# Moving the extra messages of a window from the end of its own pass to the head of the next one

## The reference

```python
h = (x @ W).reshape(n_nodes, Hh, Cc)
alpha = leaky_relu(a_src[src] + a_dst[dst])
m = jax.ops.segment_max(alpha, dst, num_segments=n_nodes)
e = jnp.exp(alpha - m[dst])
denom = jax.ops.segment_sum(e, dst, num_segments=n_nodes)
w = e / jnp.clip(denom, 1e-16)[dst]
out = jax.ops.segment_sum(w[:, :, None] * h[src], dst, num_segments=n_nodes)
```

## Time and profile before

| | |
|---|---|
| median of three runs | 6508.33 us |
| the profiled execution | 6517.74 us, its span 6515.9 us |
| PE busy | 4981.0 us (76%) |
| DVE busy | 5313.4 us (82%) |
| ACT busy | 2717.7 us (42%) |
| POOL busy | 4585.1 us (70%) |
| mean granted clock of PE | 0.775 of full |

### The profile page before, as it was taken

The page is one execution under the profiler, slowest core; times in us unless marked ns, Lnnn a source line. Parts: engine busy times, 40 slices in busy tenths (PEclk is TensorE's granted clock), DMA queues, the critical chain, the costliest instruction groups (busy, mean ns, idle before and its releaser), DMA issues. The chain is left out here.

```text
span 6515.9 us, 110173 instructions
## 1 busy us (share of the span) xinstructions
PE 4981.0 (76%) x21652; PEld 3682.0 (57%) x21653; DVE 5313.4 (82%) x16735; ACT 2717.7 (42%) x4351; POOL 4585.1 (70%) x4837
## 2 busy tenths in 40 slices
PE   6788888888888577777777777758778778787876
PEld 5555655555556355555555555536656556566653
DVE  6788888888888788888888888877778778777788
ACT  3333333333333245554545455533333333333335
POOL 2777777777776577776767676737777777777764
PEclk8777877877777678777777777767777777778786
DMA  8555555555555455555555555535555555555545
GB/s 274 149 156 156 157 157 155 157 156 156 156 155 141 117 162 160 160 159 156 159 158 162 153 162 157 162 102 161 160 158 161 160 159 161 160 160 160 160 131 159
DMA packets 505894, 1027.11 MB, mean 158 GB/s; under 512 B 146891, under 2 KB 313199, under 8 KB 504878
## 3 DMA queue, kind: packets, MB, share of 16 engines
q0 software_dynamic: 226208, 633.50, 36.2%
q1 hardware_dynamic: 278798, 382.44, 18.1%
HBM read 931.37 MB, written 84.15 MB: 156 GB/s over the span
## 5 line engine op out<-in xcount | busy, mean ns | idle before, releaser
L1032 POOL DMA_INDIRECT e_rows<-table,loaded x4689 | 4489.2, 957 | 1756.8 <-issue 1392.6
L1266 PE MATMUL e_p_mm<-e_rows,e_onehot 128*128 128x264 f32 x9378 | 2466.5, 417 | 0.0
L1266 PEld LDWEIGHTS e_p_mm<-e_rows,e_onehot 128*128 128x128 f32 x9378 | 1876.3, 208 | 360.5 <-issue 20.1
L1444 DVE TENSOR_TENSOR e_rows<-e_rows,e_p_pair 128x1024 f32<-128x1024 f32 x1173 | 1417.8, 1209 | 0.0
L1436 DVE TENSOR_TENSOR e_onehot<-e_col,e_p_pair 128x512 f32<-128x512 f32 (+1 forms) x1467 | 953.4, 650 | 328.2 <-issue 280.4
L1259 PE MATMUL e_p_mm<-e_xmsg,e_onehot 128*128 128x264 f32 x1764 | 875.3, 669 | 103.3 <-ACT e_p_mm L1133 86.2
L1274 PE MATMUL e_p_one<-ad_parts,e_onehotT 128*128 x5586 | 707.8, 188 | 149.6 <-issue 143.3
L1225 ACT ACTIVATE e_rows<-e_gap 128x64 f32<-128x64 f32 (+1 forms) x294 | 80.6, 274 | 1621.0 <-DVE e_gap L1766 1614.7
L1274 PEld LDWEIGHTS e_p_one<-ad_parts,e_onehotT 128*128 128x128 bf16 x5586 | 550.4, 102 | 330.4 <-issue 193.3
L1139 ACT ACTIVATE e_onehotT<-e_onehotT,minus_pidx 128x2432 bf16<-128x2432 bf16 x294 | 681.0, 2316 | 42.0 <-DMA e_pass<-pass_rows 42.0
L1142 ACT ACTIVATE e_onehotT<-e_onehotT,one_col 128x2432 bf16<-128x2432 bf16 x294 | 682.6, 2322 | 9.6
(11 more groups left out here) (326 smaller groups left out, 5819.3 us busy)
## 6 DMA issues: line engine op xcount, KB each, us to landing
e_onehotT<-rel_rows SPq DMA_DIRECT2D x294, 608.0 KB
e_rows<-table,loaded POOLq DMA_INDIRECT x4689
e_own_row<-table SPq DMA_DIRECT2D x196, 128.0 KB
table<-e_rows_out SPq DMA_DIRECT2D x98, 132.0 KB
table<-n_rows_out SPq DMA_DIRECT2D x14, 910.0 KB, 15.6
table<-e_rows_out SPq DMA_DIRECT2D x98, 130.0 KB
n_inputs<-in_x_turned SPq DMA_DIRECT2D x14, 896.0 KB, 11.2
e_mask<-mask_rows SPq DMA_DIRECT2D x196, 64.0 KB
```

The source lines that it names most:

```text
L1032: pool.indirect_dma_start(rows[k][:, g, 0:TW], None, table[L], bass.IndirectOffsetOnAxis(ap=idx[k][:, g:g + 1], axis=0)).then_inc(s_gat[k] ...
L1266: ins = nc.tensor.matmul(p_mm[:, bass.ds(region, MW)], onehot[:, g, :], rows[k][:, g, :], start=False, stop=True, skip_group_check=True)
L1444: return nc.vector.tensor_tensor(feats, feats, p_e[:, gs, :].unsqueeze(3).to_broadcast([P, n, H, C]), ALU.mult)
```

## The change

`extras()` of a window is no longer the last thing of the window's own pass but the first DVE work of the next one, behind the table loads of that pass; the words `slots` are read there as well, and no longer ahead of `quarters(3)`. Its buffer and its semaphore counts are those of the window before. The last window's extra messages are made behind the loop.

```diff
                     if not first:
                         off, = words(dve, WINDOW_ROW, (w - 1) * WIN, 1, (PLACES - 1) * ACC_W)
+                        slots = words(dve, WINDOW_ROW, (w - 1) * WIN + W_TILE, EXTRAS, G - 1)
                         if not second:
                             offs = words(dve, WINDOW_ROW, (w - 2) * WIN, REGIONS, (PLACES - 1) * ACC_W)
                     flag, = words(dve, WINDOW_ROW, w * WIN + W_FLAG, 1, 2)
...
+                    if not first:
+                        extras((k - 1) % BUFS, slots, past, ago(2))
                     dve.wait_ge(s_ld[two], count(dve, used(u, i, TURNS) * N_LOAD))
 
                     dve.wait_ge(st["srcT"], now)
...
-                    slots = words(dve, WINDOW_ROW, w * WIN + W_TILE, EXTRAS, G - 1)
                     quarters(3)
                     if CARRY:
                         carried(w, u, i)
-                    extras(k, slots, now, past)
...
                 offs = words(dve, WINDOW_ROW, (WINDOWS - 1) * WIN, REGIONS, (PLACES - 1) * ACC_W)
+                slots = words(dve, WINDOW_ROW, (WINDOWS - 1) * WIN + W_TILE, EXTRAS, G - 1)
                 flag, = words(dve, WINDOW_ROW, (WINDOWS - 1) * WIN + W_OWN, 1, 1)
+                extras(k, slots, done, done - 1)
                 rescale(offs[0], done)
```

## The result

| | before | after |
|---|---|---|
| median, run side by side | 6509.72 us (6507.12 to 6517.74, 4 runs) | 6581.49 us (6576.14 to 6583.16, 4 runs) |
| ratio | | 1.0107, 95% interval [1.0089, 1.0125] |
| profiled execution, its span | 6517.74, 6515.9 us | 6571.58, 6569.8 us |
| mean granted clock of PE | 0.775 | 0.780 |

The change makes the kernel 72 us slower by the medians (54 by the two profiled executions). The forecast was 6556 us in a range up to 6578: the side and the place are right, the size is not. Of the executions of the kernel before that ran beside the experiments, one took 11598 us and stands in no ratio.

What follows compares the result with a forecast made beforehand. POOL was taken to bound the first and third layers, DVE's order the second. Second layer +39, first +8, third 0 and tails +1 gave +48 us, put on the median: 6556 us, the forecast's own range 6538 to 6572, 8-in-10 range 6522 to 6578.

Steps and rivals of the forecast that it cites:

- What bounds each layer: POOL's gathers pace the first and third layer at 20.1 to 20.3 us a window; DVE's order the second, 21.5 us.
- rival A: Loads ahead of the extras run while carried() still waits, both gaps vanish: second layer -120 us, 6388 us; chance 0.06.
- rival B: Slots' load takes 0.755 us for its old place, not its three words; 0.35 in the new: 6512 us; chance 0.10.
- First and third layer, tails: First layer +8 us, DVE passing POOL by 0.12 us a window; third layer 0; tails behind the loops about +1.
- The second layer's +39 us: Second layer: five ordinary windows at +0.51 us and one turn's end at +0.1 average 0.44 us, times 88 windows.
- The ordinary window: Second layer: four loads open 2.1 us ahead of the extras, less gaps of 0.76 and 0.83 saved: +0.51 us.
- Rival C: Second stop of 0.8 us stays open at turns' ends, and a moving 0.18 us stop is added: 6590 us; chance 0.10.
- A turn's end: Second layer, window at the loop's branch: 7.77 us from L1554 to scan, less 7.0 and 0.76: called +0.1 us.
- The median: The +48 us from the profile was put on the median, 9.4 us below the profiled execution: 6556 us, not 6566.

Runs made afterwards that it cites:

- e1: The change, with the slots' tiles read as four aligned words, the fourth unused, in place of three; 6534.6 us, ratio 1.0032.
- c1_before: The kernel before once more, nothing changed; 6512.9 us, ratio 0.9996.
- c0_change: The change once more, no edit; 6580.0 us, ratio 1.0103 to the kernel before.
- e12: The change, but the slots' load stays ahead of the last quarter in five of six windows, so only the extras move; 6563.6 us, ratio 1.0077.
- e5c: Kernel before, slots' load moved behind quarters(2), three opening loads read at the end of the window before in five of six windows; 6419.8 us, ratio 0.9857.
- e3: The change, with the four loads behind the last quarter's message of the window before, ahead of carried(), in five of six windows; 6453.3 us, ratio 0.9909.

## Why the prediction was right, and where it was wrong

**What bounds each layer: right.** Every edit that moved DVE's loads or its extras moved the second layer, by up to 154 us between two kernels, and left the third between 1977 and 1983.

**The loads don't run ahead (rival A): right.** They start behind the start of the last instruction of `carried()`, at 3568.5 against 3568.35, and the four stood open in every ordinary window of the second layer. The Trainium skill (Perfetto Trace Analysis, section Per-instruction lifecycle, part DVE / Act Engine Instruction) has the sequencer ready for the next instruction once one is in the wait queue; for a table load behind a waiting DVE instruction these rows disagree.

**The size of the slots' load (rival B): right.** 749 ns in its new place; four words gave back 45 us. The forecast went from SP's one pair of loads; the third load of that series, 1.063 us for four words, shows that the first word's place counts as well, which changes nothing for this load, since its three words and the four of e1 start at the same place.

**First and third layer, tails: right.** From c1_before to c0_change, two profiles with third layers of one length, the first layer grew by 6.4 us (+8 forecast; 9.3 in the first pair of profiles), the third by -0.7 (0), the rest by 0.3 (+1).

**The second layer's +39 us: the step that failed**, a mis-sized term. The same pair of profiles has +55.5 us, and the mean window 22.12 - 21.50 = 0.62 us in place of 0.44. It was wrong in two of its parts:

- *The ordinary window*, +0.51 forecast. The five of a turn average 21.41 us against 20.76, +0.64. The gap ahead of the extras is 2.22 us where I had 2.1, and the gap ahead of the scan was worth 0.72 + 0.08 and not 0.75 + 0.08: 2.22 - 0.76 - 0.80 = 0.66. The gap ahead of the extras was the sum of four loads at the length that they have in the kernel before, and there the rows were typical: none of the 336 loads of that loop is more than 40 ns longer. In the change one of the four is longer by 0.08 to 0.35 us in four of the turn's five ordinary places, and only in the fifth is the gap the 2.1 us of the forecast; in e12 none is (all by the medians). So the wrong step was to take the loads' old length for their new place. Rival C's second half had a stop that comes and goes and adds 0.15 us a window; an addition of 0.11 us a window came, from a cause that stays open. By e12 both halves of the change cost more than forecast: the extras' place 0.51 us where the sum has 0.42, the load 0.14 where it has 0.09.
- *A turn's end*, +0.1 forecast. The window with it takes 25.95 us against 25.50, +0.45 (+0.28 in the first profile of after). The stop behind the branch averages 3.6 and 3.8 us over the 13 turns in the two profiles of the change and 3.3 and 3.2 in those of the kernel before, where I had left it at 3.55 on both sides; why it is longer behind the change is not shown. The Trainium skill (Runtime: NRT & Kernel Launch, section Instruction fetch mechanics) says that a taken branch to a target outside the two pages that are loaded must wait until the target's page has been fetched. The traces have the stop, and a transfer of the queue "instruction" starts within it in 9 to 13 of the 13 turns, but they don't say which engine it is for.

(5 x 0.64 + 0.45) / 6 x 88 = 54 us, close to the measured 55.5. Of the 15 us that this is above the forecast, the ordinary windows bring 10 and the turns' ends 5.

**The median.** The second layer's term is not all of the miss. With 61.5 us in place of 48, as the profiles of c1_before and c0_change stand apart, the forecast would have been 6570, inside its range; the measured median is 12 us above that. The medians of the two kernels stand 66 to 72 us apart, the profiled executions 54 to 61.5. In both pairs the profiled execution of the kernel before was slow for its kernel (6517.7 of 6507 to 6518; 6517.3 of 6507 to 6517, and of up to 6520 counting the executions beside it), and that of the change was the fastest of its own (6571.6 and 6578.8 against 6576 to 6583). The forecast took a difference that the profile gives and put it on the median; laid on the profiled execution it would have been 6566. Which part of an execution makes these 5 to 18 us is not settled, since only the profiled ones have a trace.

## What to carry to other kernels

Where an engine's own instruction stream is the bound, scalar table loads are part of it: put each behind an instruction of that engine that has queued work, and ahead of one that must wait. Count how much that work covers (1.2 us covered three loads in e5c and not four in e3), and do not move work away from the loads that it covers. A sequencer instruction can be longer in a new place than in its old one, so a sum made of such rows needs a margin on the side of longer: here it was 0.13 us in a window of 21. At a branch back, work that is queued ahead of it covers part of its stop; ask what stands there before moving it behind.

## What the runs showed of the hardware

- A table load of three words takes 0.75 us on DVE, one of one word 0.31, one of four words at a multiple of four 0.35. Reading one word more is worth 45 us of the changed kernel.
- On SP a load of four words takes 0.46 to 0.49 us where its first word stands at a multiple of four in the table, and 1.03 to 1.07 where it does not (second layer's loop, kernel before).
- DVE's loads start only when the instruction ahead of them that waits has started: 0.12 us behind its start in the window shown.
- Loads of the same form are up to 0.35 us longer (median) in some windows of a turn in one kernel and not in another that has them at the same place of the code; neither the place alone nor the transfers of the queue "instruction" account for it.
- DVE's sequencer stood 3.2 to 3.8 us (mean) behind the branch at the end of a turn.
- Two chips ran this kernel at 9.65 and 9.72 ms (medians) in place of 6.51. The busy time of each engine in the kernels profiled there is within 2% of that on the faster chips; the cause is not known.
